# Attention steps 2 to 4 reordered around the second tile's gate and up units, and the later weights copied in five parts

## Chip, core and metric

One NeuronCore of a Trainium2 chip runs the whole program. The metric is the device time of one execution in microseconds. PE is TensorE, ACT is ScalarE, DVE is VectorE, POOL is GpSimd, and SP is the engine that issues the DMAs.

## What is computed

The input has 2 batches of 2048 tokens of 256 channels. Two branches work on the same normalised input and are added to it:

```python
xn = layernorm(x)
# branch 1: linear attention block
x = xn + dwconv(xn, cpe1)
y = ln(x); act_res = silu(y @ actp_w + b)
xi = silu(dwconv(y @ in_w + b, dwc))
q, k = elu(xi @ qk_w + b) + 1
kv = rope(k)^T xi / n;  attn = rope(q) kv / (q . mean(k)) + dwconv(xi, lepe)
x = x + attn * act_res @ out_w + b;  x = x + dwconv(x, cpe2)
branch1 = x + gelu(ln(x) @ fc1 + b) @ fc2 + b
# branch 2: gated network with integer-like (ternary) weights and a scale per row
h = silu(xn @ w1) * (xn @ w2)
branch2 = gelu(gelu(h @ h1) @ h2) @ w3
out = x_in + branch1 + branch2
```

## The kernel before

The tokens are cut into 8 tiles of 512, four to a batch. Activations are split into a high part, which the fast matmul format holds exactly, and a low part, the rest; a product with a dense weight is three matmuls, one with a ternary weight two. Every engine has its own program, written out as loops in Python; semaphores order them, and an engine never runs an instruction before the one written ahead of it.

The first half of the program is a loop over `P1_STEPS`, -1 to 9. Step i works on several tiles at once. On PE, in this order (`first_half`, L2143): `in_proj(i+1)`, `v_tokens(i-2)`, `k_proj(i-1)`, `a_channels(i+3)`, `add_kv(i-2)`, `act_proj(i+1)`, `norm_tokens(i+2)`, `q_proj(i-1)`, `norm_back(i+2)`. The other engines serve these:

- *Normalisation of tile i+2.* `norm_tokens` transposes to token rows; DVE takes the statistics (`norm_moments`), POOL the inverse deviation (`inverse_deviation(.., "b")`, `rs_b`), DVE the offsets (`norm_offsets`, `nb_b`), ACT applies them (`apply_norm`, `xnt`), `norm_back` transposes back, ACT takes the high part (`high_of_norm`, `pb_hi`), DVE the low one (`low_of_norm`, `pb_lo`), and the next step's `in_proj` reads both.
- *Input of tile i+4.* DVE takes statistics of the loaded tile (`xn_moments`), POOL the deviation (`rs_a`), DVE applies it (`apply_xn`, `xt`); `a_channels` transposes it in the next step.
- *Keys and queries of tile i-1.* DVE adds the bias to k (`bias_k`), ACT takes exp (`exp_k`, `kx`), POOL clips it (`clip_k`), and in the next step DVE forms elu (`elu_k`), which `add_kv` reads. ACT takes exp and relu of q (`exp_q`, `relu_q`), both from the bank X, and DVE forms elu of q (`elu_q`) in the next step; SP then saves q (`save_q`). `v_tokens` overwrites X and waits for the last of exp and relu; `copy_v` copies it out, and `a_channels` waits for that copy.
- *Convolutions.* For each, ACT applies the centre tap (`conv1_centre`, `conv2_centre`), DVE the left and right ones (`conv1_side`, `conv2_side`, False is left). `norm_tokens(i+2)` waits for both sides of the first one. After the second, ACT takes silu (`silu_v`) and DVE the high part (`high_of_v`, `pd_hi`).

Between these stand units of the second branch for the first four tiles, set by the table `FRONT_ROOM` (L125): at each place (`after_a1`, `after_a2`, `after_q`, `after_back1`, `after_back2`) a number of units. A unit is one of 8 chunks of the gate and up products (G0 to G7 below) or of the hidden layer (H0 to H7). A G unit is 8 matmuls; then ACT takes silu of the gate, DVE multiplies and takes the high part (`full`, `u_hi`), POOL the low part (`u_lo`). H7 of the first tile and G0 to G7 of the second one fall into steps 2, 3 and 4. ACT must hold the right table for silu, gelu or exp, and loads it where two neighbouring calls need different ones (`ACT_TABLE_LOAD`); relu, copies and scaled additions need none of their own.

Weights of the second branch come from DRAM through a ring of six pieces of 512 KB (`ring`). SP writes all 22 pieces to a scratch tensor `w_s` beside that; the last ten (`w_s[STREAM:]`) are needed only in the second half of the program (`load_block`), and before the change one DMA copies them in step 1.

## Time and profile before

| | us |
|---|---|
| median of 3 runs | 1089.48 (1087.17 to 1090.39) |
| the profiled execution | 1087.63 |
| its span, first to last instruction | 1085.80 |
| PE busy | 1029.8 (95%) |
| DVE busy | 762.9 (70%) |
| ACT busy | 593.5 (55%) |
| POOL busy | 234.3 (22%) |
| DMA moved | 180.68 MB, mean 166 GB/s |

The engines run beside one another, so the busy times don't add. A row in order of time gives start, duration, engine, line, operation, what is written from what, the number of instructions merged into it, and in brackets the idle time ahead and whose signal ended it. A row of a window gives its length and, for each engine, busy time and the number of instructions, then the granted clock of PE (1.00 is full), the DMA engines' busy share and the bytes they moved per second. Ends of matmuls are modelled and overlap with the next start.

### The profile page before, as it was taken

To read this page: it belongs to the slowest core of one execution; us is meant where nothing else is said; L and a number is where in the kernel's file an instruction comes from. 1 tells how busy PE (TensorE), PEld (TensorE's weight loads), DVE (VectorE), ACT (ScalarE), POOL (GpSimd) and SP (SyncE) were. 2 spreads that over 40 slices of the span, in tenths; PEclk is the share of its full clock that TensorE was granted. 3 is DMA by queue.
4 is the path that set the end of the run, shared out by engine and by line. 5 is a ranking of instruction groups with operands and counts; after the bars stand their busy time and mean duration, and the time that the engine had idled before them with its cause. 6 is when DMAs were issued, how large, how long until landed. Compare 5 with 4: busy or idle time off the path is not lost. (4 is left out here: it accounts for less than half of the span.)

```text
span 1085.8 us, 17166 instructions
## 1 busy us (share of the span) xinstructions
PE 1029.8 (95%) x6636; PEld 913.3 (84%) x6636; DVE 762.9 (70%) x974; ACT 593.5 (55%) x853; POOL 234.3 (22%) x208
## 2 busy tenths in 40 slices
PE   3699988999999999999999999999999999999997
PEld 3477876888777877778888889899899999999997
DVE  6775678644645668988887647768787968777664
ACT  4356766676625346456545545655556644655444
POOL 2254344331523221100111012213200211101100
PEclk9799999999999899999999999999999999999999
DMA  8869953555596455332332293152495423222210
GB/s 323 318 244 346 346 189 117 194 165 166 169 351 221 136 184 189 123 132 80 130 116 78 86 335 122 59 175 100 150 347 200 144 90 117 88 76 92 96 40 21
DMA packets 68338, 180.68 MB, mean 166 GB/s; under 512 B 4976, under 2 KB 26096, under 8 KB 64624
## 3 DMA queue, kind: packets, MB, share of 16 engines
q1 hardware_dynamic: 68256, 179.56, 47.7%
q8 instruction: 55, 0.90, 0.3%
q14 instruction: 27, 0.22, 0.1%
HBM read 121.86 MB, written 66.06 MB: 173 GB/s over the span
## 5 line engine op out<-in xcount | busy, mean ns | idle before, releaser
L2090 PE MATMUL pr<-xp_hi,wb 128*128 128x256 f32 x1344 | 320.0, 282 | 0.9 <-DVE u L1842 0.7
L2090 PE MATMUL pr<-xp_lo,wb 128*128 128x256 f32 x1344 | 319.5, 281 | 0.0
L2090 PEld LDWEIGHTS pr<-xp_hi,wb 128*128 128x128 f32 x1344 | 255.2, 190 | 2.7 <-issue 2.7
L2090 PEld LDWEIGHTS pr<-xp_lo,wb 128*128 128x128 f32 x1344 | 256.1, 191 | 0.0
L2090 PE MATMUL pr<-u_hi,ring 128*128 128x512 f32 x256 | 102.5, 401 | 1.0 <-POOL u_lo L897 1.0
L2090 PE MATMUL pr<-u_lo,ring 128*128 128x512 f32 x256 | 100.1, 391 | 0.0
L1321 ACT CAST xp_hi<-tf 128x1024 fp32r<-128x1024 f32 x48 | 50.2, 1046 | 56.5 <-PE pr L2090 20.0
L1005 POOL TENSOR_TENSOR ot<-ot,yg 128x512 f32<-128x512 f32 x14 | 25.2, 1800 | 244.3 <-DVE ot L1873 244.3
L1695 DVE TENSOR_TENSOR h_lo<-hf,h_hi 128x512 fp32r<-128x512 f32 x64 | 54.8, 863 | 32.6 <-ACT h_hi L1261 32.6
L2259 PE MATMUL pr<-wf_hi,h_hi 128*128 128x256 f32 x256 | 75.3, 294 | 0.6 <-DVE h_lo L1695 0.6
L1836 DVE TENSOR_TENSOR xp_lo<-tf,xp_hi 128x1024 fp32r<-128x1024 f32 x48 | 60.8, 1266 | 20.2 <-ACT xp_hi L1321 20.1
L2259 PE MATMUL pr<-wf_hi,h_lo 128*128 128x256 f32 x256 | 72.2, 282 | 0.0
L2259 PE MATMUL pr<-wf_lo,h_hi 128*128 128x256 f32 x256 | 72.1, 282 | 0.0
L1261 ACT ACTIVATE hf<-pr,fb 128x512 f32<-128x512 f32 x64 | 44.1, 689 | 38.6 <-PE pr L194 35.1
L2090 PE MATMUL pr<-wd,a_hi 128*128 128x256 f32 x256 | 60.6, 280 | 1.2 <-DVE a_lo L1866 1.2
L2090 PE MATMUL pr<-wd,a_lo 128*128 128x256 f32 x256 | 60.4, 279 | 0.0
L2090 PEld LDWEIGHTS pr<-u_hi,ring 128*128 128x128 f32 x256 | 48.1, 188 | 13.5 <-issue 2.3
L897 POOL TENSOR_TENSOR u_lo<-full,u_hi 128x512 fp32r<-128x512 f32 x32 | 43.8, 1374 | 66.6 <-DVE u_hi L1553 66.6
L2090 PE MATMUL pr<-xg_hi,ring 128*128 128x512 f32 x128 | 53.6, 418 | 4.5 <-ACT silu L1133 3.3
L1337 ACT ACTIVATE u<-u,prm 128x256 f32<-128x256 f32 x96 | 41.0, 498 | 30.1 <-DVE u L1862 15.1
L2090 PEld LDWEIGHTS pr<-u_lo,ring 128*128 128x128 f32 x256 | 48.1, 188 | 10.5 <-issue 0.7
L194 PE MATMUL pr<-pm_hi,wf_hi 128*128 128x512 f32 x128 | 53.3, 417 | 2.1 <-DVE pm_lo L1689 0.5
(224 smaller groups left out, 2520.8 us busy)
## 6 DMA issues: line engine op xcount, KB each, us to landing
ring<-w_s SPq DMA_DIRECT2D x42, 512.0 KB, 5.3
uf<-h_s SPq DMA_DIRECT2D x16, 1024.0 KB, 5.0
wb<-s_s SPq DMA_DIRECT2D x8, 1024.0 KB, 9.2
stage<-w_gated SPq DMA_DIRECT2D x4, 1536.0 KB, 11.7
wb<-w_s SPq DMA_DIRECT2D x6, 1024.0 KB, 10.0
vw<-v_s SPq DMA_DIRECT2D x8, 514.0 KB, 6.6
xt<-x SPq DMA_DIRECT2D x8, 512.0 KB, 7.3
xn_s<-xh SPq DMA_DIRECT2D x8, 512.0 KB, 9.8
```

The lines of the kernel that those rows point to most:

```text
L194: last = e.matmul(out, w(k), v(k), start=(k == 0 and n == 0), stop=(k == chunks - 1 and n == 2))
L897: pool.tensor_tensor(u1_lo[:, m, :], full1[:, m % 2, :], u1_hi[:, m, :].bitcast(F32), ALU.subtract) \
L1005: pool.tensor_tensor(ot[:, part, :], ot[:, part, :], yg[:, part, :], ALU.add).then_inc(s["out_sum"], 1)
L1261: last = e.activation(out_, F1[:, m % 2, :], ACT.Gelu, bias=fb[:, m:m + 1])
L1321: e.copy(xp_hi[p][:], sources[p]).then_inc(s["u_hi"], 1)
L1337: last = e.activation(results[k][:, m, :], source[:, m, :], ACT.Gelu, scale=par(scale, RESULTS[k][0] * HB + m))
L1695: e.tensor_tensor(h_lo[:, m, :], hf[:, m % 2, :], h_hi[:, m, :].bitcast(F32), ALU.subtract) \
L1836: e.tensor_tensor(xp_lo[p][:], sources[p], xp_hi[p][:].bitcast(F32), ALU.subtract).then_inc(s["u_lo"], 1)
L2090: return e.matmul(bank, w.bitcast(dt), v_.bitcast(dt), start=first, stop=last, skip_group_check=True)
L2259: last = e.matmul(as_tokens(F2)[:, n, :], h[:, k, cols], w[:, k, :], start=(k == 0 and j == 0), stop=(k == KH - 1 and j == 2))
```

## The change

Nothing is computed differently. Instructions trade places in steps 2, 3 and 4 of the first half on all engines, and one DMA becomes five.

```diff
+KEPT_LATE = (3, 4, 5, 6, 7)
...
-              for place, gates, hidden in (("after_a1", 1, 1), ("after_a2", int(i in (0, 1, 3, 7, 8)), 0), ("after_q", 1, 1 + (i == 0)),
+              for place, gates, hidden in (("after_a1", 1, 1), ("after_a2", int(i in (0, 1, 2, 3, 7, 8)), 0), ("after_q", int(i != 2), 1 + (i == 0)),
...
-                if i == 1:
-                    sp.wait_ge(s["w_kept"], 32)
-                    sp.dma_start(w_s[STREAM:], w_gated[STREAM:]).then_inc(s["w_kept"], 16)
+                if i in KEPT_LATE:
+
+                    if i == KEPT_LATE[0]:
+                        sp.wait_ge(s["w_kept"], 32)
+                    first = STREAM + KEPT_LATE.index(i) * (PIECES - STREAM) // len(KEPT_LATE)
+                    last = STREAM + (KEPT_LATE.index(i) + 1) * (PIECES - STREAM) // len(KEPT_LATE)
+                    sp.dma_start(w_s[first:last], w_gated[first:last]).then_inc(s["w_kept"], 16)
...
+                front("p", i, "after_a1", between=(lambda: inverse_deviation(i + 2, "b", "b_applied")) if i == 4 else None)
...
+                if i in (2, 3):
+                    inverse_deviation(i + 4, "a", "a_applied")
+                if valid(i - 1) and i != 3:
                     clip_k(i - 1)
...
+                if i == 3:
+                    clip_k(i - 1)
...
+                if i == 4:
+                    exp_k(i - 2)
+                if i in (3, 4):
+                    conv1_centre(i + 2)
                 if valid(i):
                     conv2_centre(i)
...
+                if i in (2, 3):
+
+                    front("p", i, "after_a2")
                     apply_norm(i + 2)
+                    relu_q(i - 1, second=False)
+                    front("p", i, "after_q")
                     high_of_norm(i + 2)
+                    front("p", i, "after_back1")
+                    front("p", i, "after_back2")
+                    exp_q(i - 1, second=True)
+                    if i == 2:
+                        exp_k(i - 1)
...
+                if i in (3, 4):
                     copy_v(i - 2)
                     elu_k(i - 2)
+                    conv1_side(i + 2, False)
                     conv2_side(i, False)
+                    bias_k(i - 1)
+                    conv1_side(i + 2, True)
                     conv2_side(i, True)
...
+                if i == 4:
+                    front("p", i, "after_a1")
+                if valid(i + 2) and i == 2:
+                    norm_offsets(i + 2, "b", "b_applied")
                 front("p", i, "after_a2")
...
+                if i in (3, 4):
+                    elu_q(i - 2)
...
+                    if i == 4:
+
+                        front(wide, "p", i, "after_a1")
                     if valid(i + 3) and i >= 2:
                         a_channels(i + 3)
```

In words: in step 2, G0 moves from behind `q_proj(1)` to ahead of it. In steps 2 and 3, ACT takes relu of q first, the units' silus together, and exp of q last; exp of k(1) follows at the end of step 2, exp of k(2) at the start of step 4. The centre taps of tiles 5 and 6 move to the start of steps 3 and 4. DVE copies v and forms elu of k first in steps 3 and 4, the right taps of the second convolution after those of the first, elu of q late. In step 4, PE runs G7 ahead of `a_channels(7)`, and DVE serves it after the statistics of tile 6. On POOL, the clip of k goes behind the deviation of the next input tile, in step 3 behind all else.

ACT in step 2, from the gelu of H7 (the first `silu_108`, with its table load) to the xi of tile 4. Before:

```order
L1125 ACT_TABLE_LOAD
L1125 ACTIVATE silu_108<-pr,prm 128x512
L1013 ACTIVATE x_82<-xh_81,prm,w1p 128x512 x2
L1051 ACT_TABLE_LOAD
L1051 ACTIVATE kx<-kt 128x1024
L1013 ACTIVATE xnt<-pr,nb_b,rs_b 128x256 x4
L1059 ACTIVATE qe<-pr,prm 128x512 x2
L1133 ACT_TABLE_LOAD
L1133 ACTIVATE silu_108<-pr,prm 128x512
L1077 CAST pb_hi<-pr 128x1024
L1133 ACTIVATE silu_108<-pr,prm 128x512
L1063 ACTIVATE q<-pr,prm 128x512 x2
```

And now, to the load for exp at the end of the step (`q` is relu, `qe` exp of q, `kx` exp of k):

```order
L1148 ACT_TABLE_LOAD
L1148 ACTIVATE silu_108<-pr,prm 128x512
L1156 ACT_TABLE_LOAD
L1156 ACTIVATE silu_108<-pr,prm 128x512
L1026 ACTIVATE xnt<-pr,nb_b,rs_b 128x256 x4
L1085 ACTIVATE q<-pr,prm 128x512 x2
L1100 CAST pb_hi<-pr 128x1024
L1156 ACTIVATE silu_108<-pr,prm 128x512
L1077 ACT_TABLE_LOAD
L1077 ACTIVATE qe<-pr,prm 128x512 x2
L1064 ACTIVATE kx<-kt 128x1024
```

Both silus of the step come under one load, and both exps stand behind the high part.

DVE at the end of step 3 and in the first part of step 4, from the application to the input tile 7 on. Before:

```order
L1429 TENSOR_SCALAR xt_79<-xt_79,mv_a_68,rs_a_71 128x256 x4
L1548 SCALAR_TENSOR_TENSOR full1_109<-pr2,prm_49,silu1_108 128x512
L1553 CAST u1_hi_106<-full1_109 128x512
L1446 SCALAR_TENSOR_TENSOR x0_82<-xh0_80,prm_49,x0_82 128x512 x2
L1514 COPY vt_100<-pr0 128x8x128
L1501 SCALAR_TENSOR_TENSOR kt_92<-kt_92,kx_93 128x1024
L1506 SCALAR_TENSOR_TENSOR q_99<-qe_98,q_99 128x1024
L1446 SCALAR_TENSOR_TENSOR v0_96<-xi0_94,prm_49,v0_96 128x512 x4
L1496 TENSOR_TENSOR kt_92<-pr1,kb_52 128x1024
L1446 SCALAR_TENSOR_TENSOR x0_82<-xh0_80,prm_49,x0_82 128x512 x2
```

Now:

```order
L1469 TENSOR_SCALAR xt_79<-xt_79,mv_a_68,rs_a_71 128x256 x4
L1588 SCALAR_TENSOR_TENSOR full1_109<-pr2,prm_49,silu1_108 128x512
L1593 CAST u1_hi_106<-full1_109 128x512
L1554 COPY vt_100<-pr0 128x8x128
L1541 SCALAR_TENSOR_TENSOR kt_92<-kt_92,kx_93 128x1024
L1486 SCALAR_TENSOR_TENSOR x0_82<-xh0_80,prm_49,x0_82 128x512 x2
L1486 SCALAR_TENSOR_TENSOR v0_96<-xi0_94,prm_49,v0_96 128x512 x2
L1536 TENSOR_TENSOR kt_92<-pr1,kb_52 128x1024
L1486 SCALAR_TENSOR_TENSOR x0_82<-xh0_80,prm_49,x0_82 128x512 x2
L1486 SCALAR_TENSOR_TENSOR v0_96<-xi0_94,prm_49,v0_96 128x512 x2
```

The copy of v and elu of k have moved ahead of the first left tap, elu of q has left this place, and the right taps of the second convolution stand last.

PE in step 4, from the last products of `k_proj(3)` on. Before, the transposes of tile 7 follow at once:

```order
L194 MATMUL pr<-wq_hi,pd_hi 128x256
L194 MATMUL pr<-wq_lo,pd_hi 128x256
L194 MATMUL pr<-wq_hi,pd_lo 128x256
L180 MATMUL pr<-identity,xt 128x128 x8
L2068 MATMUL pr<-vt,kt 128x129 x8
```

Now the eight matmuls of G7 (four shown) stand between:

```order
L196 MATMUL pr<-wq_hi,pd_hi 128x256
L196 MATMUL pr<-wq_lo,pd_hi 128x256
L196 MATMUL pr<-wq_hi,pd_lo 128x256
L2146 MATMUL pr<-xg_hi,ring 128x512
L2146 MATMUL pr<-xg_lo,ring 128x512
...
L2146 MATMUL pr<-xg_hi,ring 128x512
L2146 MATMUL pr<-xg_lo,ring 128x512
L182 MATMUL pr<-identity,xt 128x128 x8
L2124 MATMUL pr<-vt,kt 128x129 x8
```

G7 has left its place behind `act_proj(5)`.

## Rows read from the trace of the kernel before

**Rows 1.** The page: busy time, share of the span and instructions of PE.

```profile
PE 1029.8 (95%) x6636; PEld 913.3 (84%) x6636; DVE 762.9 (70%) x974; ACT 593.5 (55%) x853; POOL 234.3 (22%) x208
```

**Rows 2.** Windows: steps 2, 3 and 4, cut at the starts of in_proj.

```profile
119.70:148.28 28.58, 25.23 (x142) 20.62 (x141) 17.89 (x38) 20.12 (x26) 9.32 (x11) 0.99 0.93 326
148.28:178.36 30.08, 28.14 (x148) 23.13 (x149) 24.65 (x45) 20.75 (x30) 14.06 (x13) 0.95 0.36 126
178.36:209.20 30.84, 27.90 (x150) 23.79 (x148) 22.60 (x41) 18.22 (x26) 13.79 (x15) 0.94 0.44 155
```

**Rows 3.** PE in order of time, steps 2 to 4: all that waited.

```profile
142.61 1.09 PE L180 MATMUL pr<-identity,xnt 128*128 128x128 f32 x8 [0.88 <-ACT xnt L1013]
...
145.75 0.49 PE L2090 MATMUL pr<-xg_hi,ring 128*128 128x512 f32 x1 [1.11 <-ACT silu L1133]
...
148.28 0.77 PE L194 MATMUL pr<-pb_hi,wq_hi 128*128 128x512 f32 x1 [1.33 <-DVE pb_lo L1519]
...
164.71 1.09 PE L187 MATMUL pr<-identity,x 128*128 128x128 f32 x8 [0.75 <-DVE x L1446]
...
175.49 0.50 PE L2090 MATMUL pr<-xg_hi,ring 128*128 128x512 f32 x1 [1.12 <-ACT silu L1133]
...
188.08 1.40 PE L180 MATMUL pr<-identity,xt 128*128 128x128 f32 x8 [2.82 <-DVE vt L1514]
```

**Rows 4.** Windows of 4 us in which PE's granted clock is low.

```profile
148.00:152.00 4.00, 3.72 (x11) 2.99 (x12) 3.60 (x12) 2.37 (x4) 1.98 (x3) 0.61 0.38 135
188.00:192.00 4.00, 3.92 (x21) 3.91 (x22) 3.87 (x5) 1.01 (x1) 1.41 (x4) 0.58 0.24 97
352.00:356.00 4.00, 4.00 (x23) 4.00 (x22) 4.00 (x2) 0.00 (x0) 3.64 (x2) 0.56 0.07 27
```

**Rows 5.** ACT in order of time, step 2, and act of tile 5 in step 4.

```profile
138.39 1.28 ACT L1051 ACT_TABLE_LOAD   x1
139.68 1.07 ACT L1051 ACTIVATE kx<-kt 128x1024 f32<-128x1024 f32 x1
140.65 1.91 ACT L1013 ACTIVATE xnt<-pr,nb_b,rs_b 128x256 f32<-128x256 f32 x4
142.44 1.28 ACT L1059 ACTIVATE qe<-pr,prm 128x512 f32<-128x512 f32 x2
...
145.60 1.01 ACT L1077 CAST pb_hi<-pr 128x1024 fp32r<-128x1024 f32 x1
147.84 0.69 ACT L1133 ACTIVATE silu<-pr,prm 128x512 f32<-128x512 f32 x1 [1.23 <-DMA h_s<-silu]
...
195.42 0.69 ACT L1097 ACTIVATE act<-pr,ab 128x512 f32<-128x512 f32 x1 [0.65 <-PE pr L194]
```

**Rows 6.** DVE in order of time, steps 2 to 4.

```profile
122.72 1.38 DVE L1429 TENSOR_SCALAR xt<-xt,mv_a,rs_a 128x256 f32<-128x256 f32 x4 [1.43 <-POOL rs_a L863]
...
146.92 1.22 DVE L1519 TENSOR_TENSOR pb_lo<-pr,pb_hi 128x1024 fp32r<-128x1024 f32 x1
...
169.07 1.25 DVE L1439 SCALAR_TENSOR_TENSOR nb_b<-mv_b,rs_b 128x4 f32<-128x4 f32 x1 [0.18 <-POOL rs_b L863]
...
181.04 3.32 DVE L1429 TENSOR_SCALAR xt<-xt,mv_a,rs_a 128x256 f32<-128x256 f32 x4 [0.34 <-POOL rs_a L863]
...
185.39 1.41 DVE L1446 SCALAR_TENSOR_TENSOR x<-xh,prm,x 128x512 f32<-128x512 f32 x2
```

**Rows 7.** SP's DMA issues in order of time: duration is that of the issue.

```profile
110.87 13.26 SPq L504 DMA_DIRECT2D x_s<-x  x1
...
137.70 0.48 SPq L554 DMA_DIRECT2D h_s<-silu  x1
```

**Rows 8.** POOL in order of time, and one DVE row beside the clip.

```profile
169.01 1.30 POOL L897 TENSOR_TENSOR u_lo<-full,u_hi 128x512 fp32r<-128x512 f32 x1
...
280.13 2.76 POOL L892 TENSOR_SCALAR kx<-kx 128x1024 f32<-128x1024 f32 x1
...
281.07 0.43 DVE L1553 CAST u_hi<-full 128x512 fp32r<-128x512 f32 x1
```

More of the change, by code:

```diff
@@ L902, in low_of_xg, with front @@
                 pool.tensor_tensor(x_lo[:], xf, x_hi[:].bitcast(F32), ALU.subtract).then_inc(s["x_split"], 1)
-            def front(*where):
+            def front(*where, between=None):
                 for n in FRONT.get(where, ()):
@@ L909, in front @@
                     if not hidden and m == KH - 1:
+                        if between is not None:
+                            between()
                         low_of_u(n)
@@ L939, in _ @@
                 front("p", i, "after_q")
-                if valid(i - 1):
+                if i in (2, 3):
+                    inverse_deviation(i + 4, "a", "a_applied")
+                if valid(i - 1) and i != 3:
                     clip_k(i - 1)
-                if valid(i + 4):
+                if valid(i + 4) and i not in (2, 3):
                     inverse_deviation(i + 4, "a", "a_applied")
@@ L1051, in exp_k, with q_free @@
                 e.activation(kx[:], kt[:], ACT.Exp).then_inc(s["d_kexp"], 1)
-            def exp_q(i):
+            def q_free(i):
                 e.wait_ge(s["d_qprod"], i + 1)
@@ L1057, in exp_q, with relu_q @@
                     e.wait_ge(s["q_saved"][i % 2], slot_count(i - 2))
+            def exp_q(i, second=False):
+                if not second:
+                    q_free(i)
                 for k in range(KC):
-                    e.activation(qe[:, k, :], X[:, k, :], ACT.Exp, bias=par("q_b", k))
-            def relu_q(i):
+                    last = e.activation(qe[:, k, :], X[:, k, :], ACT.Exp, bias=par("q_b", k))
+                if second:
+                    last.then_inc(s["d_qparts"], 1)
+            def relu_q(i, second=True):
+                if not second:
+                    q_free(i)
                 for k in range(KC):
                     last = e.activation(q[:, i % 2, k, :], X[:, k, :], ACT.Relu, bias=par("q_b", k))
-                last.then_inc(s["d_qparts"], 1)
+                if second:
+                    last.then_inc(s["d_qparts"], 1)
             def apply_norm(i):
@@ L1581, in _ @@
                 front("p", i, "first")
-                if valid(i + 2) and i >= 0:
-                    conv1_side(i + 2, False)
-                if valid(i - 2):
+                if i in (3, 4):
                     copy_v(i - 2)
                     elu_k(i - 2)
-                    elu_q(i - 2)
-                if valid(i):
+                    conv1_side(i + 2, False)
                     conv2_side(i, False)
+                    bias_k(i - 1)
+                    conv1_side(i + 2, True)
                     conv2_side(i, True)
-                if valid(i - 1):
-                    bias_k(i - 1)
-                if valid(i + 2) and i >= 0:
-                    conv1_side(i + 2, True)
-                front("p", i, "after_a1")
+                else:
+                    if valid(i + 2) and i >= 0:
+                        conv1_side(i + 2, False)
+                    if valid(i - 2):
+                        copy_v(i - 2)
+                        elu_k(i - 2)
+                        elu_q(i - 2)
+                    if valid(i):
+                        conv2_side(i, False)
+                        conv2_side(i, True)
+                    if valid(i - 1):
+                        bias_k(i - 1)
+                    if valid(i + 2) and i >= 0:
+                        conv1_side(i + 2, True)
+                if i != 4:
+                    front("p", i, "after_a1")
                 if ends_batch(i - 2):
@@ L1599, in _ @@
                     norm_moments(i + 2)
+                if i == 4:
+                    front("p", i, "after_a1")
+                if valid(i + 2) and i == 2:
+                    norm_offsets(i + 2, "b", "b_applied")
                 front("p", i, "after_a2")
-                if valid(i + 2) and i >= 0:
+                if valid(i + 2) and i >= 0 and i != 2:
                     norm_offsets(i + 2, "b", "b_applied")
@@ L1604, in _ @@
                     high_of_v(i)
+                if i in (3, 4):
+                    elu_q(i - 2)
                 front("p", i, "after_q")
@@ L2158, in first_half @@
                         act_proj(i + 1)
-                    if i != 0:
+                    if i not in (0, 4):
                         front(wide, "p", i, "after_a1")
```

38 lines of the change are left out of this document (20 added, 18 removed).

## Prediction

> **What bounds the kernel now.** I read the page first: PE is busy 95% of the span [rows 1], so only PE's idle time and its slow time can go, about 56 us in all. Then I cut the span at the starts of steps 2, 3 and 4 [rows 2]. They last 28.6, 30.1 and 30.8 us. Then PE in order of time, keeping the instructions that had to wait [rows 3]: 0.88, 1.11 and 1.33 us in step 2, 0.75 and 1.12 in step 3, 2.82 in step 4, together 8.0. Last the granted clock [rows 4]: it is at its upper level (2.4 GHz) except from 148 to 152 (mean 0.61) and from 188 to 192 (0.58). What is missing from full clock there is 0.39 x 4 = 1.6 and 0.42 x 4 = 1.7 us. So steps 2 to 4 hold 8.0 + 3.3 = 11.3 us that are not work: the most the reordering can give. No PE work is removed.
>
> The waits end on ACT and DVE, not on matmuls. ACT's queue shows why [rows 5]: between the statistics of tile 4 and its high part it runs a table load (1.28), exp of k (1.07), exp of q (1.28) and another load; G1's silu then waits 1.23 for a store of the hidden layer. DVE's low part of tile 4 starts at 146.92 and ends at 148.14 [rows 6], and PE's in_proj(4) starts at 148.28 [rows 3].
>
> **Step 2.** norm_back(4) stays where it is. Its chain (norm_tokens, statistics on DVE, deviation on POOL, offsets, ACT's normalisation 140.65 to 142.56 [rows 5]) is not shortened: ACT would be free earlier without exp of k and the centre tap, but the offsets come only then. G0 ahead of q_proj(1) swaps two pieces of PE work, so the wait of 0.88 stays. What follows changes. ACT now runs relu of q (as long as exp, 1.28) and then the high part; norm_back(4) starts at 142.61 and takes 1.09 [rows 3], so the high part (1.01) runs 143.75 to 144.8. DVE did G0's product earlier and is free: the low part, 1.22, ends at 146.05. in_proj(4) starts at 146.2 instead of 148.28: **2.1 us gained**. PE itself is ready at 145.4 and waits 0.8.
>
> This needs G1's silu to be no hindrance. Its store was issued at 137.70 [rows 7], and silu went on at 147.84, when it had landed [rows 5]. SP was held 13.26 us at one issue while the copy of ten weight pieces filled the queue [rows 7]. Without that copy in step 1 I take the store to land before 145. If it doesn't, exp of q comes at 151 instead of 148 and v_tokens(1), which waits for it, costs 2.
>
> **Step 3.** PE's work: 30.08 less 1.87 of waits, 1.6 of clock and 0.3 of restarts (some 0.15 each) is 26.3. New waits:
> - ACT ends the step before with silu of G1, a load (1.28), exp of q (1.28) and exp of k (1.07): 144.8 + 0.69 + 3.63 = 149.1. Only then come the two halves of xi(4), 0.69 each, to 150.5. k_proj(2) needs them and PE is there at 150.0 (in_proj's end plus v_tokens): 0.5.
> - DVE: after the low part the tile-6 statistics, G1's product and the application to xt of tile 6, between 1.4 and 3.3 [rows 6], then copy_v(1) and elu_k(1), of the low part's size, 1.2 each (elu_k waits for POOL's clip, exp of k's end plus 2.76 [rows 8] = 151.9), left taps of both convolutions 2 x 1.41, bias_k 1.2, right taps of tile 5 1.41. That is 158.8 undisturbed, 161 with what POOL takes; PE reaches norm_tokens(5) at 160.8: 146.2, the 16.43 from in_proj(4) to it before [rows 3], less 0.75 of wait and 1.6 of clock, plus the 0.5. No wait, or little.
> - The second convolution's right taps (1.41) and G2's product with its cast (1.2) now stand between norm_tokens(5) and the statistics. If DVE is at 161 they delay the offsets: 161 + 2.6 + 3.3 for statistics and POOL's deviation (before, from the transposes' end 164.71 + 1.09 [rows 3] to 169.07 [rows 6]) = 166.9. The offsets op took 1.25 us for four columns at 169.07, ending with POOL's u_lo (169.01 to 170.31) [rows 6, 8]; so 168.1, and the normalisation, 1.91 [rows 5], gives norm_back(5) at 170.1. PE is ready at 168.2, 7.4 after norm_tokens (from 164.71 to 175.49, less 1.12 of wait and norm_back and half a unit, some 2.2): 1.9. If DVE was done at 158.8 this is 0 to 0.5.
> - relu of q(2), 1.28, G4's silu and the high part come behind, so G5's second half waits 0 to 0.4 and in_proj(5) 0.5.
>
> Sum 27.4 to 28.7. DVE was hit by POOL in the same place before [rows 6], so I take 28.3: **1.8 gained**, nearly all of it the clock.
>
> **Step 4.** copy_v(2) no longer stands behind the left tap (1.41), and G7 covers the rest, so the 2.82 goes. A unit is eight matmuls, about 1.85 us: G1's second half, four of them, ran from 145.75 to 146.95 with the last one's tail [rows 3]. Late next is elu_k(2): exp of k(2) ends at 4.8 after the step's start, POOL has two u_lo and the clip (2.76) to do until 8.2, DVE holds the application to xt (3.32) and G6: elu_k ends near 9.9, PE reaches add_kv(2) at 9.5: 0.4. PE: before, from 178.36 to act_proj's end, which releases act's second half at 195.42 [rows 5], 17.0, less 2.82, 0.15 of restart and 1.7 of clock, is 12.35; with G7 14.2, with the 0.4 14.6. From there ACT sets the pace. Before, it went from the second half of act(5) at 195.42 [rows 5] to the next step at 209.20 almost without idle: 13.8. Now exp was the last table, so a silu load of 1.28 stands ahead of act(5). 0.9 of it hides before the second half, 0.4 does not. G7's silu no longer waits 0.24. silu of v waits up to 0.5 for the right taps, now after those of tile 6. 14.6 + 0.4 + 13.8 - 0.24 + 0.5 = 29.1 against 30.84: **1.7 gained**. PE's slack against ACT is gone here: norm_back(6) and in_proj(6) will wait about 1 together.
>
> The table load is weighed here. kx starts 0.01 us after a load of 1.28 ends [rows 5]. The Trainium skill, ScalarE: Activation LUTs, "What ACT_TABLE_LOAD costs", adds a drain of about 1.38 us, 2.66 in all, and asks for calls to be batched by table set; the change has one switch more. By the page the step would be 1.4 us longer, by the row not, and no drain shows here.
>
> **The queues passed.** SP's save of q(1) waits for elu_q(1), now at 168 instead of 157, and holds the saves of act(4), v(3), xn(6) and the ring load of G3. The ring is six pieces deep and the piece that G3 frees is read in step 5; act and v slots are asked for again two tiles later. Free. The five copies of 1 MB each in steps 3 to 7 run where DMA moves 126 and 155 GB/s [rows 2] against 326 in step 2: free as well; uncovered, one would hold what is behind it 3 to 5 us. Nothing after step 4 changes order, and PE is 95% busy, so what is gained stays.
>
> **Sum.** 2.1 + 1.8 + 1.7 = 5.6 us. The profiled execution took 1087.63 (span 1085.80): 1082.0. The median of the three runs is 1089.48, 1.85 above it, so **1083.9**. About 0.3%, 3.3 us, is what a measurement of this kernel can tell from no change.
>
> **Rivals.**
> 1. *All waits go.* DVE is ahead in step 3 and nb is not held, ACT keeps up in step 4: 8.0 + 3.3 = 11.3, that is 1078.2. For it: the copy is out of the way. Against it: the 0.88 has the same chain as before. 7 us and more: 0.13.
> 2. *The clock still falls.* Two falls came at gaps, one, at 352 to 356 (0.56), with PE 4.00 of 4.00 busy [rows 4]; so gaps don't explain them alone. Up to 2.0 of wait at norm_back(5) and 0.9 + 0.8 around 145 remain. Two falls of 1.6: 5.6 - 3.3 = 2.3, 1087.2. One fall: 1085.5, still faster. Gain below 3.3 down to none, with the store landing late in it: 0.27.
> 3. *Slower: POOL holds DVE.* clip_k(1) now starts within 0.2 us of tile 6's application to xt and can hold it 2.76; u_lo of G0 the elu_k behind (1.3), u_lo of G1 the taps (1.3), u_lo of G6 the taps of step 4 (1.3): 6.7. It decides from 5.6 on the path; with one clock fall, 1.6, the kernel is 2.7 slower, 1092.2. For it: the 1.25 and 3.32 of rows 6. Against it: a cast of DVE's took its usual 0.43 inside a clip (281.07 in 280.13 to 282.89) [rows 8], and part of DVE's lateness has slack. The Trainium skill, SBUF — State Buffer, "Who interferes with whom", gives the pair of ports to whichever starts first, for the whole instruction, where the DVE op reads two SBUF inputs or is in a two-port mode; by that u_lo's case agrees with the row, and the clip would hold elu and taps too. Slower than before: 0.08, by over 0.3%: 0.05.
> 4. *The copy alone matters.* If the orders cancel out and only G1's 1.23 goes: 1088.3. In the 0.27.
>
> **Numbers.** Forecast (gain 3.3 to 7): 0.52. Faster by over 0.3%: 0.52 + 0.13 = 0.65; within: 0.30; slower: 0.05. The range leaves out the best of rival 1 and all of rival 3: 1079.5 to 1089.5, as the last term of each step is good for some 1 us each way and a median here moves by 1.5.
>
> **What would show it.** norm_back(4) still waiting 0.8 to 0.9; in_proj(4) two us earlier; G1's silu without a DMA behind it; in step 3 the wait moved to norm_back(5), in step 4 no wait at a_channels(7), but short ones at norm_back(6) and in_proj(6); no half clock in steps 2 to 4. It is wrong if PE waits for DVE's taps (norm_tokens) or elu_k, or if a fall of the clock comes back at norm_back(5).

## The result, and the profile after

The changed kernel takes 1081.42 us (1081.06 to 1081.53) against 1089.52 (1087.17 to 1090.39): ratio 0.9933, 95% interval 0.9919 to 0.9946. It is 8 us faster by the medians, 7.3 by the ratio, and inside the range. Three executions were in a slow state (one of four of the change, 5689 us, one of six of e0, 2581, and one of twelve of e2, 1144): ranges and ratios leave them out, medians count them, which moves those by 0.3 at most. The change's profiled execution took 1081.53 (span 1079.7) against 1087.63, so the two profiles lie 6.1 us apart. In the tables below a step length is that of one profiled execution, and a ratio stands for all runs.

The page after, busy time of the engines, as [rows 1] before:

```profile
PE 1027.9 (95%) x6636; PEld 910.2 (84%) x6636; DVE 764.1 (71%) x974; ACT 594.2 (55%) x854; POOL 236.4 (22%) x208
```

The windows of steps 2, 3 and 4 of the change, in the columns of [rows 2]:

```profile
120.52:146.95 26.43, 24.95 (x141) 20.70 (x141) 18.06 (x38) 17.13 (x23) 6.59 (x10) 1.00 0.59 179
146.95:174.48 27.53, 26.59 (x148) 22.15 (x149) 24.25 (x44) 18.82 (x27) 14.78 (x13) 1.00 0.21 76
174.48:203.99 29.51, 27.21 (x150) 21.95 (x149) 23.94 (x42) 23.59 (x32) 17.94 (x16) 1.00 0.59 199
```

The steps are 2.15, 2.55 and 1.33 us shorter, together 6.03. What lies ahead of them is 0.82 longer, what lies behind them 0.9 shorter (875.7 us against 876.6); neither can be put down to the change, as step 2 begins between 118.9 and 121.3 and the part behind step 4 takes 874.9 to 876.6 in the profiles of all kernels below, 875.6 and 875.3 in two that keep the old order (e2, e3). Granted clock is 1.00 in the three steps (0.99, 0.95, 0.94 before). Outside them both profiles have half clock from 40 to about 56 and a fall near 350, of 6.8 us before and of 3.4 after. The 0.82 has to be taken off every time below before it is held against a time of the prediction.

PE in order of time, steps 2 to 4 of the change: all that waited, as [rows 3]:

```profile
143.41 1.09 PE L182 MATMUL pr<-identity,xnt 128*128 128x128 f32 x8 [0.85 <-ACT xnt L1026]
146.95 0.47 PE L196 MATMUL pr<-pb_hi,wq_hi 128*128 128x512 f32 x1 [0.60 <-DVE pb_lo L1559]
151.43 0.36 PE L196 MATMUL pr<-wq_hi,pd_hi 128*128 128x256 f32 x1 [0.57 <-issue]
169.85 1.09 PE L182 MATMUL pr<-identity,xnt 128*128 128x128 f32 x8 [0.35 <-ACT xnt L1026]
...
184.26 1.06 PE L182 MATMUL pr<-identity,xt 128*128 128x128 f32 x8 [1.01 <-DVE vt L1554]
190.41 1.09 PE L189 MATMUL pr<-identity,x 128*128 128x128 f32 x8 [0.25 <-DVE x L1486]
198.58 1.09 PE L182 MATMUL pr<-identity,xnt 128*128 128x128 f32 x8 [0.41 <-ACT xnt L1026]
203.99 0.47 PE L196 MATMUL pr<-pb_hi,wq_hi 128*128 128x512 f32 x1 [0.63 <-DVE pb_lo L1559]
```

4.7 us of waiting are left of 8.0, at other places: norm_back(4), in_proj(4), k_proj(2), norm_back(5), a_channels(7), norm_tokens(6), norm_back(6), in_proj(6).

ACT in order of time at the end of step 2, as [rows 5]:

```profile
143.23 1.28 ACT L1085 ACTIVATE q<-pr,prm 128x512 f32<-128x512 f32 x2
144.53 1.01 ACT L1100 CAST pb_hi<-pr 128x1024 fp32r<-128x1024 f32 x1
145.96 0.69 ACT L1156 ACTIVATE silu<-pr,prm 128x512 f32<-128x512 f32 x1 [0.41 <-DMA h_s<-silu]
```

SP's issues of the change, as [rows 7]:

```profile
111.72 0.53 SPq L506 DMA_DIRECT2D x_s<-x  x1
...
138.55 1.28 SPq L556 DMA_DIRECT2D h_s<-silu  x1
```

The issue that had held SP 13.26 us takes 0.53. The store that G1's silu needs is issued at 138.55, and silu, which waits for it, starts at 145.96, 7.4 us later against 10.1 before [rows 5, 7].

DVE in order of time, step 3 of the change, as [rows 6]:

```profile
145.58 1.22 DVE L1559 TENSOR_TENSOR pb_lo<-pr,pb_hi 128x1024 fp32r<-128x1024 f32 x1 [2.23 <-ACT pb_hi L1100]
...
149.93 2.16 DVE L1469 TENSOR_SCALAR xt<-xt,mv_a,rs_a 128x256 f32<-128x256 f32 x4 [0.30 <-POOL rs_a L869]
152.01 1.22 DVE L1554 COPY vt<-pr 128x1024 f32<-128x1024 f32 x1
153.15 2.24 DVE L1541 SCALAR_TENSOR_TENSOR kt<-kt,kx 128x1024 f32<-128x1024 f32 x1
155.31 1.40 DVE L1486 SCALAR_TENSOR_TENSOR x<-xh,prm,x 128x512 f32<-128x512 f32 x2
...
159.09 1.40 DVE L1486 SCALAR_TENSOR_TENSOR x<-xh,prm,x 128x512 f32<-128x512 f32 x2
```

The same stretch before, with elu of q and all the taps of the second convolution ahead of the right taps `x` that norm_tokens(5) needs:

```profile
154.89 1.21 DVE L1514 COPY vt<-pr 128x1024 f32<-128x1024 f32 x1
156.03 1.21 DVE L1501 SCALAR_TENSOR_TENSOR kt<-kt,kx 128x1024 f32<-128x1024 f32 x1
157.16 1.22 DVE L1506 SCALAR_TENSOR_TENSOR q<-qe,q 128x1024 f32<-128x1024 f32 x1
158.29 3.91 DVE L1446 SCALAR_TENSOR_TENSOR v<-xi,prm,v 128x512 f32<-128x512 f32 x4
...
163.25 1.40 DVE L1446 SCALAR_TENSOR_TENSOR x<-xh,prm,x 128x512 f32<-128x512 f32 x2
```

The measure used below is this queue's length, from the end of the low part to the end of those right taps. Before it is 164.65 - 148.14 = 16.5 us, after 160.49 - 146.80 = 13.7.

DVE at the start of step 4 of the change:

```profile
177.41 4.03 DVE L1469 TENSOR_SCALAR xt<-xt,mv_a,rs_a 128x256 f32<-128x256 f32 x4 [0.30 <-POOL rs_a L869]
181.37 0.74 DVE L1588 SCALAR_TENSOR_TENSOR full<-pr,prm,silu 128x512 f32<-128x512 f32 x1
182.14 0.85 DVE L1593 CAST u_hi<-full 128x512 fp32r<-128x512 f32 x1
182.91 1.21 DVE L1554 COPY vt<-pr 128x1024 f32<-128x1024 f32 x1
```

POOL in the same stretch:

```profile
177.34 2.58 POOL L903 TENSOR_TENSOR u_lo<-full,u_hi 128x512 fp32r<-128x512 f32 x2
179.90 2.81 POOL L898 TENSOR_SCALAR kx<-kx 128x1024 f32<-128x1024 f32 x1
```

### The profile page after: what moved, and what is told of

It is laid out like the page before. It is cut to its first block and busy times, and to the rows that moved or that the text cites. A ratio compares the mean times of both kernels' runs of the same rounds, so it can differ in the third digit from the quotient of the medians.

```text
span 1079.7 us, 17171 instructions
## 1 busy us (share of the span) xinstructions
PE 1027.9 (95%) x6636; PEld 910.2 (84%) x6636; DVE 764.1 (71%) x974; ACT 594.2 (55%) x854; POOL 236.4 (22%) x208
```

## The experiments

The theory after the result: of the change, the order on DVE is what pays in steps 3 and 4, the order on ACT what pays in step 2, and the five copies are needed for the latter. The rivals: the clock (what the prediction gave step 3's gain to), the copies alone, and POOL holding DVE. The table has all kernels; ratios are against before on the same chip, and as chips differ (before has medians from 1087.9 to 1088.5 beside the experiments), kernels are compared by ratio.

| kernel | median us | ratio (95%) | steps 2, 3, 4 in the profile |
|---|---|---|---|
| before | 1089.52 | | 28.58, 30.08, 30.84 |
| the change | 1081.42 | 0.9933 (0.9919 to 0.9946) | 26.43, 27.53, 29.51 |
| e0 the change again | 1081.05 | 0.9936 (0.9922 to 0.9950) | 26.43, 27.78, 29.53 |
| e1 change, one copy | 1083.35 | 0.9962 (0.9948 to 0.9976) | 26.46, 29.62, 29.49 |
| e2 before, five copies | 1089.21 | 1.0010 (0.9999 to 1.0020) | 28.60, 30.09, 30.80 |
| e3 before, wait filled | 1086.53 | 0.9987 (0.9979 to 0.9996) | 28.60, 30.10, 30.15 |
| e5 change, G7 late | 1084.25 | 0.9967 (0.9953 to 0.9981) | 26.46, 28.08, 31.82 |
| e6 change, copy_v(2) late | 1085.85 | 0.9979 (0.9966 to 0.9993) | 26.43, 28.11, 34.10 |
| e7 change, copy_v(2) first | 1080.08 | 0.9924 (0.9907 to 0.9942) | 26.43, 27.79, 28.31 |
| e8 as e7, silu load early | 1081.10 | 0.9933 (0.9915 to 0.9951) | 26.42, 28.07, 28.24 |
| e9 before, DVE's order | 1084.34 | 0.9958 (0.9945 to 0.9972) | 28.60, 28.11, 28.11 |
| e10 change, exp of k(1) early | 1082.04 | 0.9946 (0.9928 to 0.9964) | 27.05, 27.47, 29.50 |
| e11 as e7, exp of k(1) later | 1082.18 | 0.9944 (0.9928 to 0.9961) | 26.42, 29.00, 28.30 |
| e12 change, DVE's order undone | 1086.59 | 0.9990 (0.9980 to 1.0000) | 26.42, 31.48, 32.80 |

**e0: the change once more.**

> The changed kernel again, as the yardstick for the runs beside it. Theory: the kernel before pays 8.0 us of PE waits in steps 2 to 4 and two falls of the clock (about 3.3 us), the change has 4.7 us of waits and no fall there; 6 us between two profiles, 6 to 8 between medians, because the executions of before scatter by some 3 us with the falls and those of the change do not. Rival: the 8.1 us between the medians hold a part outside steps 2 to 4; then the spans of steps 5 and on differ by more than 1 us between profiles.

Steps 2 and 4 repeat to 0.02 us, step 3 to 0.25. The latter follows one wait: k_proj(2) waits 0.85 instead of 0.57. Six kernels have the same orders up to there, and in them that wait follows the store that G1's silu waits for:

| | change | e7 | e0 | e5 | e6 | e8 |
|---|---|---|---|---|---|---|
| G1's silu waits for the store | 0.41 | 0.65 | 0.70 | 0.87 | 0.91 | 0.94 |
| k_proj(2) waits | 0.57 | 0.80 | 0.85 | 1.03 | 1.05 | 1.05 |
| step 3 | 27.53 | 27.79 | 27.78 | 28.08 | 28.11 | 28.07 |

The profiled execution of the change is the fastest of the six. In step 3 less than 0.6 us is no difference between two profiles, and what the store is late comes through to PE.

The rival had a sign, over 1 us of difference behind step 4. Before and e0 do differ there by 1.35 us (876.6, 875.3), but e2 and e3, with the old order, lie at 875.6 and 875.3, so the sign doesn't speak for the rival.

**e1 and e2: the copies.** e1 is the change with the one copy in step 1 as before; e2 is the kernel before with the five copies.

```diff
-KEPT_LATE = (3, 4, 5, 6, 7)
+KEPT_LATE = (1,)
```

> The changed kernel with the copy of the ten late weight pieces in one DMA in step 1, as before. Theory: the store of hidden chunk 7 lands about 2 us later (147.8 to 148.5 on the clock of the first trace), silu of G1 waits for it, exp of q(1) comes behind and v_tokens(1) and k_proj(2) wait some 2 us more: 1.5 to 2.5 us slower than the change. Rival (the copy is free): within 0.3 us of the change. Rival 4 (the copy alone is the gain): within 1 us of the kernel before.

> The kernel before with only the copy in five parts. Theory: PE's waits in step 2 do not hang on the store (in_proj(4) waits for the low part, ahead of G1's product), so the time stays within 0.7 us of the kernel before, apart from a fall of the clock more or less (1.7 us each). Rival 4 (the copy is what counts): 1.2 us or more faster in step 2, in_proj(4) starting before 147.2 where it was 148.28.

In e1, ACT in order of time:

```profile
143.20 1.01 ACT L1100 CAST pb_hi<-pr 128x1024 fp32r<-128x1024 f32 x1
146.71 0.69 ACT L1156 ACTIVATE silu<-pr,prm 128x512 f32<-128x512 f32 x1 [2.50 <-DMA h_s<-silu]
```

and PE behind it:

```profile
150.03 1.09 PE L189 MATMUL pr<-identity,v 128*128 128x128 f32 x8 [1.39 <-ACT qe L1077]
152.18 0.36 PE L196 MATMUL pr<-wq_hi,pd_hi 128*128 128x256 f32 x1 [1.06 <-issue]
```

G1's silu stands ahead of exp of q in the change, so the store's lateness (2.50 of wait) goes through to v_tokens(1). Step 3 is 1.84 longer than in e0, and the median 2.3, as forecast (1.5 to 2.5). Without the new order the copies bring nothing: e2 is within 0.1 of before in all three steps. So the five copies are worth about 2 us, but only to the new order, as the prediction priced it.

e2 tells more. Its clock didn't fall at 148, and yet step 3 is as long as before. PE in e2:

```profile
155.86 1.06 PE L181 MATMUL pr<-identity,xt 128*128 128x128 f32 x8 [1.02 <-DVE vt L1518]
...
164.32 1.09 PE L188 MATMUL pr<-identity,x 128*128 128x128 f32 x8 [0.75 <-DVE x L1450]
```

In the profile before the first of these waits isn't there [rows 3]: PE at half clock came just as late as DVE. With the clock full it waits 1.02 for DVE instead. PE's own time in step 3, its length less its waits, is 28.21 us before and 27.20 in e2: the fall took 1.0 us of it, not the 1.6 of the prediction, as it began before in_proj(4) did, while PE waited (the clock is 0.96 from 144 to 148).

**e3: the clock in step 4 of the kernel before.** Ten matmuls whose product nobody reads run where PE waits 2.82 at a_channels(7); nothing else differs.

```diff
+                    if i == 4:
+                        filler(38, 3, 10)
                     if valid(i + 3) and i >= 2:
                         a_channels(i + 3)
```

> The kernel before with ten idle matmuls (2.2 us of work, result never read) on PE inside the 2.82 us wait ahead of the transposes of tile 7 in step 4. No wait is shortened. Theory (the fall of the clock at 189 follows from PE's idleness): the fall goes, and step 4 is 1.2 to 1.7 us shorter. Rival (the falls come whatever PE does in these 3 us, as the one at 352 with PE busy): no difference, within 0.5 us.

Windows of e3, step 4 and the 4 us that stood at 0.58 [rows 4]:

```profile
177.93:208.08 30.15, 28.89 (x159) 23.86 (x158) 22.62 (x41) 18.09 (x25) 14.16 (x15) 1.00 0.45 160
188.00:192.00 4.00, 4.00 (x30) 3.51 (x29) 3.87 (x5) 1.01 (x1) 2.19 (x4) 1.00 0.32 131
```

The fall is gone; it follows PE's idleness. But of the 1.7 us that full clock gives back only 0.69 arrives (1.2 to 1.7 were forecast), since PE then waits 0.76 for DVE's right taps at norm_tokens(6). And again there is no fall at 148 (a matter of the execution, the code up to there is that of before) and step 3 is 30.10. **In the kernel before, the half clock cost nothing in step 3 and 0.7 in step 4.**

**e9 and e12: the order on DVE, alone and undone.** e9 is the kernel before with only DVE's order of steps 3 and 4 from the change; e12 is the change with that order put back.

```diff
+                if i in (3, 4):
+                    copy_v(i - 2)
+                    elu_k(i - 2)
+                    conv1_side(i + 2, False)
+                    conv2_side(i, False)
+                    bias_k(i - 1)
+                    conv1_side(i + 2, True)
+                    conv2_side(i, True)
...
                     high_of_v(i)
+                if i in (3, 4):
+                    elu_q(i - 2)
```

> The kernel before with DVE's order of steps 3 and 4 alone taken from the change (copy of v and elu of k ahead of the left taps, the second convolution's right taps behind the first one's, elu of q late). ACT, POOL, PE, SP and the one copy stay as before. Theory (DVE's queue bounded step 3, and the half clock at 148 was hidden under it): the waits at a_channels(6) and norm_tokens(5) go. Without a fall of the clock at 148 step 3 is 28.3 us (30.1 less 1.02 and 0.75), with one 1.6 is lost again where before it cost nothing, 28.9 or more. Step 4: the wait of 2.82 at a_channels(7) shrinks by the left tap, 1.4, so 29.4. In all 2.5 to 3.3 us faster than before, ratio 0.997. Rival (ACT's new order is what pays in steps 3 and 4): steps 3 and 4 stay within 0.3 of 30.1 and 30.8.

> The change with DVE's order of the convolutions, the copy of v and both elu in steps 3 and 4 put back as before; DVE still serves G7 behind the statistics in step 4, and ACT, POOL, PE, SP and the copies stay as changed. It is the complement of e9. Theory (DVE's queue bounds steps 3 and 4, and its order is what pays there): step 2 stays 26.4; step 3 is again as long as DVE's work from the low part of tile 4 to the right taps of tile 5, 29.7 to 30.3; in step 4 the left tap, elu of q and the second convolution's right taps, 1.4 + 1.2 + 1.4, stand ahead of norm_tokens(6) again, so 31.5 to 32.5, with a wait of 2.4 at a_channels(7). In all within 0.2% of before or a little faster, ratio 0.998 to 1.000. Rival (ACT's and PE's order carry half of it by themselves, and the orders are exchangeable): steps 3 and 4 28.8 and 30.2, ratio 0.996.

Windows of e9, steps 3 and 4:

```profile
147.51:175.62 28.11, 26.65 (x149) 22.21 (x149) 23.54 (x45) 20.11 (x29) 14.71 (x13) 1.00 0.24 90
175.62:203.73 28.11, 26.49 (x149) 22.17 (x148) 21.51 (x41) 18.22 (x26) 15.09 (x15) 1.00 0.36 127
```

and of e12:

```profile
145.66:177.14 31.48, 28.34 (x148) 23.89 (x149) 25.32 (x45) 19.02 (x28) 14.14 (x13) 0.95 0.45 155
177.14:209.94 32.80, 28.13 (x150) 23.27 (x148) 25.23 (x41) 23.41 (x31) 17.58 (x16) 0.95 0.49 175
```

What e12's PE waits for in steps 3 and 4:

```profile
155.43 1.06 PE L182 MATMUL pr<-identity,xt 128*128 128x128 f32 x8 [1.98 <-DVE vt L1554]
...
187.95 1.06 PE L182 MATMUL pr<-identity,xt 128*128 128x128 f32 x8 [2.06 <-DVE vt L1554]
196.46 1.09 PE L189 MATMUL pr<-identity,x 128*128 128x128 f32 x8 [2.62 <-DVE x L1486]
```

The parts of steps 3 and 4 together, against the kernel before (60.92): DVE's order alone -4.70, everything else alone +3.36, both -3.88. Over all runs the parts look otherwise: by the ratios e9 gains 0.42% (4.6 us), e12 0.10% (1.1), the change 0.67% (7.3). DVE's queue shows both: low part to right taps of tile 5 takes 13.0 us in e9 (147.37 to 160.32), 13.7 in the change, 16.5 before and 18.3 in e12 (145.5 to 163.81; there the left tap waits 0.95 for ACT's centre tap, which now stands in this step, and takes 2.45 instead of 1.41). My theory forecast e12's step 3 at 29.7 to 30.3 and its step 4 at 31.5 to 32.5; both were worse. e9 also beat the forecast of 29.4 for step 4, as the second convolution's right taps no longer stand ahead of norm_tokens(6) either, and no fall came there. e2, e3 and e9 all have full clock in step 3, so between them DVE's order alone is worth 1.98 (30.09 and 30.10 against 28.11). What it is worth under a fall stands in no profile.

So why isn't e9 the fastest kernel? Its profiled execution (1080.96) is one of two near 1081, at a mean clock of 0.990; the other eight took 1083.6 to 1084.8 at 0.988 to 0.989. The change's runs all have 0.990 to 0.992. PE still idles 1.12 + 1.34 us at 145 and 1.48 at 184 in e9. That falls of the clock come back in those eight runs is inferred from the mean clock; which stretch they are in isn't recorded. It is no full account either: 0.990 against 0.9885 is some 1.6 us of clock by my estimate, and they are 3.3 slower. So the profile of e9 shows one of its shorter executions, and its -4.70 isn't what the kernel gains as a rule. Not tried was DVE's order with the new step 2 alone, steps 3 and 4 being left as before on ACT; by the steps it would be 26.4 + 28.1 + 28.1, no shorter than e7 below.

**e5 and e6: PE's wait at a_channels(7) in the change.** e5 puts G7 back behind act_proj(5) on PE. e6 lets DVE do six statistics that nobody reads, 2 us, ahead of copy_v(2).

```diff
-                    if i == 4:
-
-                        front(wide, "p", i, "after_a1")
...
-                    if i not in (0, 4):
+                    if i != 0:
```

```diff
+                if i == 4:
+                    e.wait_ge(s["a_moments"], TILES)
+                    for n in range(6):
+                        e.bn_stats(st["a" if n < SUB else "h"][:, n % SUB, :], xt[:, 0, n % SUB, :])
```

> The changed kernel with G7 on PE back behind act_proj(5); all other orders as changed. Theory: copy_v(2) on DVE ends at the same time, so the wait at a_channels(7), 1.01 in the change, becomes 1.01 + 1.84 = 2.85, and the clock may fall there again. Behind it ACT set the pace (waits of 0.4 and 0.6 at norm_back(6) and in_proj(6)), and G7 there fills them: step 4 is 30.3 to 30.9 us against 29.5, the kernel 0.8 to 1.5 slower than the change. Rival (the DVE order alone did it, G7's place is free): step 4 within 0.3 of 29.5.

> The changed kernel with six idle statistics instructions on DVE (0.35 us each, 2.1 together, results never read) ahead of copy_v(2) in step 4. Theory: PE's wait at a_channels(7) goes from 1.01 to 3.1, and DVE's later work follows, so step 4 is 2.0 to 2.2 us longer, and the clock falls within a few us behind the wait (none falls there in the change): up to 0.7 us more. Rival (the clock doesn't follow PE's idle time): no fall between 180 and 200.

The wait in e5:

```profile
183.27 1.12 PE L182 MATMUL pr<-identity,xt 128*128 128x128 f32 x6 [2.86 <-DVE vt L1554]
```

and the window behind it:

```profile
184.00:188.00 4.00, 4.00 (x22) 3.96 (x21) 3.03 (x6) 1.01 (x1) 2.08 (x4) 0.61 0.00 1
```

In e6 the wait is 2.97, until 186.90, and these four us run at 0.50:

```profile
188.00:192.00 4.00, 4.00 (x21) 4.00 (x20) 2.54 (x4) 1.01 (x1) 2.02 (x4) 0.50 0.00 0
```

In e5, without its cover, the wait is 2.86, that is 1.85 more than in the change: just G7's work. The step is 2.29 longer (31.82, where 30.3 to 30.9 was forecast), 0.44 more than that idle time; the waits at norm_tokens(6) and norm_back(6), 0.25 and 0.41 in the change, are gone, so part of the fall's cost took their place. In e6 1.96 us of wait make the step 4.57 longer, with a fall of 6.8 us (2.0 to 2.9 was forecast, the fall included). Here the fall does cost: 4.57 is 2.6 more than the idle time. DVE was not what held PE there, it stood idle 1.85 us for PE ahead of the bias of k. G7 ahead of a_channels(7) is worth 2.3 us.

**e7 and e8: what is left of that wait.** In the change copy_v(2) ends 9.64 us after the step's start (184.12), before it was 9.57 (187.93). The left tap of 1.41 is no longer ahead of it, but xt of tile 7 took 4.03 instead of 3.32, the cast behind it 0.85 instead of 0.43, and all began 0.25 later. e7 runs copy_v(2) ahead of that application, at the end of step 3's list. e8 is e7 with a silu of one column on ACT that makes the table load run ahead of act(5).

```diff
                 if i in (3, 4):
-                    copy_v(i - 2)
+                    if i == 3:
+                        copy_v(i - 2)
...
+                if i == 3:
+                    copy_v(i - 1)
                 if valid(i + 4):
                     apply_xn(i + 4)
```

> The changed kernel with copy_v(2) on DVE ahead of the application to the input of tile 7 at the end of step 3. In the change that application took 4.03 us because POOL's two low parts of u held it, and copy_v(2) came behind it and G6's product, though v_tokens(2) was done 4.5 us earlier. Theory: copy_v(2) (1.2, reads PSUM, not held) runs in the time in which DVE was held anyway, the wait of 1.01 at a_channels(7) goes, step 4 is 0.8 to 1.1 us shorter than 29.5. Rival (elu_k(2) and the clip on POOL bind next): the wait moves to add_kv(2), gain under 0.3.

> The kernel with copy_v(2) first, and besides a silu of one column on ACT ahead of act(5) in step 4, so that the table load (1.28 us) runs while ACT waits for PE. Theory: the load's 0.4 us on the path goes, norm_back(6) and in_proj(6) wait less: 0.3 to 0.5 us shorter in step 4 than the kernel with copy_v(2) first alone, 1.2 to 1.5 shorter than the change. Rival (the load was hidden): no difference.

DVE in e7:

```profile
178.18 1.23 DVE L1554 COPY vt<-pr 128x1024 f32<-128x1024 f32 x1 [1.27 <-PE pr L189]
179.32 2.20 DVE L1469 TENSOR_SCALAR xt<-xt,mv_a,rs_a 128x256 f32<-128x256 f32 x4
```

ACT in e8:

```profile
186.58 1.28 ACT L1192 ACT_TABLE_LOAD   x1
187.87 0.20 ACT L1192 ACTIVATE spare<-prm 128x1 f32<-128x1 f32 x1
```

e7's wait at a_channels(7) is gone and step 4 is 1.2 us shorter. DVE stands idle 1.27 us, but the application, started later, then takes 2.20 instead of 4.03: POOL's two `u_lo` (177.14 to 179.67) are nearly over. The copy of v from PSUM (178.18 to 179.41) ran beside them in its usual 1.2 us. Over all runs e7 is ahead of the change by less than the intervals (0.9924 against 0.9933 and 0.9936), so its 1.2 us is shown by the step (0.8 to 1.1 were forecast), not by the total. In e8 act(5) finds its table loaded and starts at 189.06, as soon as PE is done, and the step gains 0.07 (0.3 to 0.5 were forecast, the rival is right). Ahead of act(5) the load was not on the path: norm_tokens(6) waits 0.27 for DVE's right taps in e8 as in e7.

**e10 and e11: where exp of k(1) stands.** e10 puts it back ahead of the normalisation of tile 4; e11 (from e7) puts it behind xi of tile 4 in step 3, with DVE's left tap ahead of elu of k.

```diff
                     front("p", i, "after_a2")
+                    if i == 2:
+                        exp_k(i - 1)
                     apply_norm(i + 2)
...
-                    if i == 2:
-                        exp_k(i - 1)
```

```diff
-                if i == 4:
+                if i in (3, 4):
                     exp_k(i - 2)
...
-                    if i == 2:
-                        exp_k(i - 1)
```

> The change with exp of k(1) in step 2 back ahead of the normalisation of tile 4, where it costs ACT one more change of tables (silu of G0, load, exp, normalisation, relu, high part, load, silu of G1). Theory (what counts in step 2 is what stands on ACT ahead of the high part): ACT waited 1.62 us for the offsets there, and load and exp take 1.28 + 1.06 = 2.34, so the normalisation starts 0.7 late, norm_back(4) waits 1.5 instead of 0.85 and in_proj(4) comes 0.7 later: step 2 27.1 instead of 26.4. Behind it silu of G1 needs a load of 1.28 more, exp of k's 1.06 is gone, so k_proj(2) still waits 0.6 to 1.4. In all 0.7 to 1.5 us slower than the change. Rival (the place of exp of k is indifferent, the relu ahead of exp of q and G0 do it all): step 2 within 0.2 of 26.4.

> The change with copy_v(2) ahead of the application to tile 7, as in e7, and exp of k(1) moved from the end of step 2 behind xi of tile 4 in step 3, DVE taking the left taps between the copy of v(1) and elu of k(1). Theory (the wait at k_proj(2) is ACT's exp of k ahead of xi): that wait, 0.6 to 0.9, goes, the clip starts 1.3 later and ends near 154.3, when DVE has just done the left taps, and step 3 is 27.0 to 27.2; 0.7 faster than e7, ratio 0.9918. Rival (the clip and the u_lo behind it now hold DVE's elu and the taps instead): step 3 27.8 or more, and norm_tokens(5) or norm_back(5) waits by what k_proj(2) no longer does.

In e10 norm_back(4) waits 1.49 and step 2 takes 27.05 where 27.1 was expected: what stands on ACT ahead of tile 4's normalisation beyond its 1.62 us of idle time goes straight to the path. k_proj(2) doesn't wait, since xi of tile 4 no longer has exp of k ahead; that step 3 gets something back for it (27.47 against 27.53 and 27.78) is within the scatter. Over all runs e10 can't be told from the change. e11's forecast failed. PE:

```profile
157.21 2.05 PE L2127 MATMUL pr<-vt,kt 128*128 128x129 f32 x16 [2.10 <-DVE kt L1539]
```

k_proj(2) doesn't wait, but add_kv(1) waits 2.10 for elu of k, which started 1.2 us later in the step than in e7 (154.88, the clip ended at 154.84) and took 2.28 beside POOL's `u_lo`. Step 3 is 1.2 longer than in e7. The wait at k_proj(2), 0.80 in e7, is the cheaper one.

## Why the prediction was right, and where its steps were not

**Step 2, 2.1: measured 2.15, by the mechanism named.** in_proj(4) was forecast at 146.2; with 0.82 off it came at 146.13. norm_back(4) waits 0.85 (0.8 to 0.9 forecast), in_proj(4) 0.60 (0.8). The store landed at 145.1 in the time of before, where "before 145" was taken, and silu waits 0.41 for it; so the mark "G1's silu without a DMA behind it" did not come true, and in the other profiles of this order silu waits up to 0.94. e10 shows that the new place of exp of k carries 0.6 of the 2.15. If the store lands late, step 2 doesn't pay but step 3 does, by the 2 us forecast (e1).

**Step 3, 1.8: measured 2.3 to 2.55 in the change and e0. The size held, the reason did not.** The step of the working that failed is "nearly all of it the clock". It took 1.6 us off for the clock and 1.87 for waits, and then filled 1.9 in again at norm_back(5). The fall had taken only 1.0 us of PE's own time (e2), and e2 and e3, with the clock full at 148, gained nothing at all. e9 has DVE's order alone, at full clock, and gained 1.97. The sign stood in [rows 3]: even at half clock PE waited 0.75 for DVE's right taps at norm_tokens(5). From in_proj(4) to there the two engines take the same time, 16.43 and 16.5 us, because both ends are waits of PE for DVE. PE's own part of it was 15.7 with the fall and 14.7 without (e2: 16.45 less 1.02 and 0.75), so in the old order DVE was the later one either way. The forecast did lay DVE's new queue beside PE's, and well: 158.8 to 161, it ended at 159.7 in the time of before. What it lacked is the same comparison for the old order, which would have given DVE's order the gain. The term that was too large is the wait at norm_back(5), 1.9 forecast, 0.35 measured: DVE was taken at 161 and was 1.3 ahead, which brought norm_back(5) to 169.0 instead of 170.1, and PE came 0.5 later than forecast. The wait at k_proj(2), 0.5 forecast and 0.57 measured, is luck in part: 0.41 of it is the store, which the sum put at nothing, and with the store later it is 0.80 to 1.05. The upper end of the sum, 28.7, leaves out its own last item (0 to 0.4 and 0.5); neither wait came.

**Step 4, 1.7: measured 1.33.** The term that failed is "copy_v(2) no longer stands behind the left tap (1.41), and G7 covers the rest, so the 2.82 goes". G7 covered 1.85, as a unit was sized. The left tap's 1.41 gave nothing, because DVE met POOL's `u_lo` and clip ahead of it: 1.01 is left, and e7 takes it away. A second error hid part of the first: 0.5 was added for silu of v, which waits for nothing. The forecast waits at norm_back(6) and in_proj(6), "about 1 together", are 0.41 and 0.63. add_kv(2) doesn't wait (0.4 forecast). norm_tokens(6) waits 0.25 for DVE's taps, small, but a wait that the prediction had named as a sign that it is wrong. By the table load the step was to lose 0.4; e8 shows 0.07. The rule of the Trainium skill, ScalarE: Activation LUTs, "What ACT_TABLE_LOAD costs", that was weighed there (a drain of about 1.38 us with each load) doesn't show: in e8 the next activation starts 0.01 us after the load's end, and in the change the load at 146.67 starts 0.02 after the silu ahead of it.

**From the steps to the median.** The forecast was 2.5 us high. 0.4 of it is the steps. The other 2 is the 1.85 that was added because the profile before lay that much under its median. The change's profile lies at its median. Before spread over 1085.2 to 1091.5 us in the runs of the experiments, with mean clocks of 0.983 to 0.991, the low ones in the longer runs; the eight runs of the change and e0 spread over 1079.7 to 1082.3 at 0.990 to 0.992. So the change seems to take away scatter as well, and an offset that came from it should not have been carried over. The gain of 8.1 between the medians therefore lies above the 3.3 to 7 that had most of the chances, where only rival 1 stood, with 0.13, whose mechanism didn't come; by the ratio it is 7.3, with an interval (5.9 to 8.8) that reaches into both. In the steps, 6.03, the forecast holds.

**The rivals.** All waits gone (1078.2): no, 4.7 are left. The clock still falls: not in steps 2 to 4; the fall near 350 is there before and after, 6.8 us long in one kernel and 3.4 in another whatever the order. POOL holds DVE: it happened at four places, but for less than priced. elu of k(1) took 2.24 (1.0 more than before), the offsets 1.24 (1.25 before), xt of tile 6 2.16 (1.38 by itself, but 2.35 before), xt of tile 7 4.03 (0.7 more than before). What came through to PE is the last one, 1.01 at a_channels(7), and of the offsets' 1.24 at most the 0.35 at norm_back(5). The copy alone matters: no, e2 is 1.001. The mark "no half clock in steps 2 to 4" came true, but isn't proof of the reason that it was meant for.

## What to carry to other kernels

A fall of PE's clock costs only what it makes PE later than the engine that PE waits for next: 0 in step 3 and 0.7 in step 4 of the kernel before, but 2.6 in e6. Before crediting PE's idle or slow time, take PE's own time (without its waits) from one wait for an engine to the next, and that engine's queue between the same events. Here it was 15.7 against 16.5, so making PE faster alone could not pay. A reorder over several engines is best judged with each engine's part alone and the rest alone, and by all runs, not by one profile of each: in the profiles DVE's part gave more than the whole in its steps (-4.7 against -3.9), and the rest was a loss (+3.4) without it; over all runs the whole gains more (7.3 us) than DVE's part (4.6).

A large copy between two DRAM tensors belongs where no short store is waited for. Cutting it up and moving it to later steps was worth 0 in one order and 2 us in another; which of the two did it was not tried apart.
